# Making the projection's first chunk ready beside attention's last head

## The reference

```
ada = silu(c) @ W_ada + b_ada                     # six vectors of 576 for each of the 2 samples
h = modulate(layernorm(x), shift_msa, scale_msa)
q, k, v = split(h @ W_qkv + b_qkv)
o = softmax(q * 36**-0.5 @ k.T) @ v               # per head
x = x + gate_msa * (o @ W_proj + b_proj)
h = modulate(layernorm(x), shift_mlp, scale_mlp)
x = x + gate_mlp * (gelu(h @ W_fc1 + b_fc1) @ W_fc2 + b_fc2)
```

## Time and profile before

| what | value |
|---|---|
| median of 3 runs | 3662.12 us (3662.05 to 3669.55) |
| profiled execution, its own time | 3666.17 us |
| its span, first to last instruction | 3664.4 us |
| mean granted TensorE clock | 0.980 |
| TensorE busy | 3529.4 us (96%) |
| VectorE busy | 1886.7 us (51%) |
| ScalarE busy | 1560.5 us (43%) |
| GpSimd busy | 350.4 us (10%) |

### The profile page before, as it was taken

One profiled execution on the slowest core, in us unless ns is written; L12 is line 12 of the kernel. 1 busy time (PEld: TensorE's weight loads), 2 busy tenths in 40 slices (PEclk: granted clock), 3 DMA queues, 4 the chain that ended last, 5 costly groups with the idle time before them and its releaser, 6 DMA issues. The chain is left out here.

```text
span 3664.4 us, 46431 instructions
## 1 busy us (share of the span) xinstructions
PE 3529.4 (96%) x16996; PEld 2264.3 (62%) x16996; DVE 1886.7 (51%) x3413; ACT 1560.5 (43%) x2903; POOL 350.4 (10%) x277
## 2 busy tenths in 40 slices
PE   5999989999999999999999999997869999999999
PEld 4888844444444444444444444435759898988988
DVE  4445546666666666666666666624543323332232
ACT  2233246666665555665556555563551101111010
POOL 0000000111100000000000000005421010100000
PEclk8999989999999999999999999998989999999999
DMA  4455332121212111111112121105753222422221
GB/s 151 154 173 169 108 83 51 35 61 38 54 32 48 32 48 33 39 43 37 46 28 51 29 51 28 32 6 167 251 204 110 91 75 81 135 89 97 67 89 49
DMA packets 146160, 289.96 MB, mean 79 GB/s; under 512 B 18242, under 2 KB 44098, under 8 KB 139024
## 3 DMA queue, kind: packets, MB, share of 16 engines
q1 hardware_dynamic: 145940, 286.99, 25.5%
HBM read 181.52 MB, written 104.34 MB: 78 GB/s over the span
## 5 line engine op out<-in xcount | busy, mean ns | idle before, releaser
L965 DVE TENSOR_REDUCE q_mx<-b_sp 128x1 f32<-128x512 f32 x1984 | 1208.7, 681 | 627.9 <-PE b_sp L913 627.8
L1001 ACT ACTIVATE b_pt<-b_st 128x512 f32<-128x512 f32 x2048 | 1031.0, 624 | 805.7 <-PE b_st L931 805.7
L942 PE MATMUL b_op<-b_pt,b_vs 128*37 128x512 f32 x4096 | 929.4, 596 | 0.0
L913 PE MATMUL b_sp<-b_ks,b_qs 108*128 108x512 f32 x1344 | 572.5, 427 | 8.5 <-DMA b_ks<-qkl 7.6
L942 PEld LDWEIGHTS b_op<-b_pt,b_vs 128*37 128x37 f32 x4096 | 223.4, 113 | 537.9 <-issue 460.0
L931 PE MATMUL b_st<-b_qs,b_ks 110*128 110x512 f32 x1344 | 520.4, 409 | 1.8 <-ACT b_pt L1001 1.8
L1631 ACT ACTIVATE d_af<-d_pf,d_b 128x512 f32<-128x512 f32 x144 | 99.3, 690 | 749.2 <-PE d_pf L1553 749.1
L913 PEld LDWEIGHTS b_sp<-b_ks,b_qs 108*128 108x128 f32 x1344 | 254.3, 189 | 203.3 <-issue 168.4
L931 PEld LDWEIGHTS b_st<-b_qs,b_ks 110*128 110x128 f32 x1344 | 252.0, 188 | 151.7 <-ACT b_pt L1001 120.7
L1570 PE MATMUL d_pm<-d_vl,d_ah 128*128 128x288 f32 x1152 | 340.8, 296 | 0.0
L1571 PE MATMUL d_pm<-d_vh,d_al 128*128 128x288 f32 x1152 | 340.5, 296 | 0.0
(11 more groups left out here) (194 smaller groups left out, 4103.8 us busy)
## 6 DMA issues: line engine op xcount, KB each, us to landing
d_hh<-hth SPq DMA_DIRECT2D x16, 1280.0 KB, 6.5
qkh<-a_th SPq DMA_DIRECT2D x72, 256.0 KB, 2.0
qkl<-a_tl SPq DMA_DIRECT2D x72, 256.0 KB, 2.3
d_yi<-y SPq DMA_DIRECT2D x64, 288.0 KB, 3.0
d_hl<-htl SPq DMA_DIRECT2D x16, 1024.0 KB, 8.8
b_qs<-qkh SPq DMA_DIRECT2D x42, 288.0 KB
b_ks<-qkh SPq DMA_DIRECT2D x42, 288.0 KB
vd<-a_vx SPq DMA_DIRECT2D x8, 1184.0 KB, 6.3
```

Source lines behind the costliest of these rows:

```text
L913: e.matmul(sp[slot % 3][:, :], qs[i][0:108, qb * 128:qb * 128 + 128], ks[i][0:108, k4 * 512:k4 * 512 + 512], start=True, stop=True).then_i ...
L942: ins = e.matmul(op[blk % 2][64 * a:64 * a + VW, :], vs[h % 2][:, 2 * j + a, :], pt[g % NP][:, a * 512:a * 512 + 512], start=j == 0, stop= ...
L965: e.tensor_reduce(mx[:, k // 4, k % 4:k % 4 + 1], sp[slot % 3][:, :], AX.X, ALU.max).then_inc(s_mx, 1)
L1001: e.activation(pt[g % NP][:, a * 512:a * 512 + 512], st[x % 3][:, :], ACT.Exp, scale=SCALE).then_inc(s_p, 1)
```

## The change

Chunk 0's turns, its split and its bias additions move out of the projection and into attention's last head. `LAST` is step 248, the last head's first. In steps 249 to 253 TensorE makes one turn each, behind the 8 scores and ahead of the 16 products, in a bank of `sp`; VectorE multiplies, in place; ScalarE rounds behind the step's exponentials and evacuation. In steps 250 to 254 GpSimd adds a bias (the first four) and subtracts a low part, the first subtraction after a wait for the last reader of `qs0`. VectorE makes `sel` in step 248. GpSimd makes the pattern `who` (now in `x1`, which is still unused) and the gated bias at attention's start, from two bias loads there. SyncE loads chunk 0's tokens in step 246, and its x in step 249 once `sel` is complete. Attention no longer waits for its last stores; the projection does, in front of `load_sums(1)`. The tiles and semaphores that both phases use move into `Prefetch`. From the projection `turn(0) + bias(0)` are removed, and its first loads begin with chunk 1. What is computed is unchanged.

```diff
 class Prefetch:
+        self.sel = S.sb("sel", [48, KT, 128], R)
+        self.gb = S.sb("gb", [128, 2, C])
+        self.oi = S.sb("oi", [128, KT, CH])
+        self.x1 = S.sb("x1", [128, 4, C])
+        self.ah = S.sb("ah", [128, KT, CH], R)
+        self.al = qs0[:, :].rearrange("p (k t) -> p k t", k=4)
+    def load_tokens(self, e, c, oi, ot):
+        cols = slice(c * CH, (c + 1) * CH)
+        e.dma_start(oi[:, 0:4, :], ot[0:512, cols].rearrange("(k p) t -> p k t", p=128)).then_inc(self.s_a[c % 2], 16)
+        for r in (0, 64):
+            e.dma_start(oi[r:r + 64, 4, :], ot[512:C, cols]).then_inc(self.s_a[c % 2], 16)
+    def load_x(self, e, c, x1, xf):
+        rows = slice(c * CH, (c + 1) * CH)
+        e.dma_start(x1[:, :, :], xf[rows, :].rearrange("(t p) c -> p t c", p=128)).then_inc(self.s_x[c % 2], 16)
...
 def phase_attention
+    LAST = NBAT - 8
+        if LAST < b <= LAST + KT:
+            s.turn, s.turn_slot = b - LAST - 1, len(slots)
+            slots.append(("turn", s.turn))
+            elif kind == "turn":
+                e.wait_ge(W.s_u, n + 1)
...
     sync
             e.dma_start(W.gt[:, b, :], gd[0, b, :].partition_broadcast(128)).then_inc(W.s_gt, 16)
+            e.dma_start(W.gb[:, b, :], b_proj.partition_broadcast(128)).then_inc(W.s_bc, 16)
+            if s.b == LAST - 2:
+                W.load_tokens(e, 0, W.oi, ot)
+            elif s.b == LAST + 1:
+                e.wait_ge(W.s_sel, 5)
+                W.load_x(e, 0, W.x1, xf)
-            e.wait_ge(s_o[i], 32 * NBLK // 2)
+        e.wait_ge(W.s_a[0], 48)
+        e.wait_ge(W.s_x[0], 16)
+        e.wait_ge(W.s_bc, 32)
     tensor
+        def turn(kt, slot):
+            e.wait_ge(W.s_sel, 5)
+            e.wait_ge(W.s_rr, 32 * HCH)
+            slot_free(e, slot)
+            e.matmul(sp[slot % 3][:, :], W.sel[:, kt, :], W.rr[:, 0, :], start=True, stop=True).then_inc(W.s_ta, 1)
+            if s.turn is not None:
+                turn(s.turn, s.turn_slot)
     vector
+            if s.b == LAST:
+                select()
+            if s.turn is not None:
+                e.wait_ge(W.s_ta, s.turn + 1)
+                e.wait_ge(W.s_a[0], 48)
+                e.tensor_tensor(W.oi[:, s.turn, :], sp[s.turn_slot % 3][:, :], W.oi[:, s.turn, :], ALU.mult).then_inc(
+                    W.s_u, 1)
     scalar
+            if s.turn is not None:
+                e.wait_ge(W.s_u, s.turn + 1)
+                e.activation(W.ah[:, s.turn, :], W.oi[:, s.turn, :], ACT.Copy).then_inc(W.s_ah, 1)
     gpsimd
+        def low(kt):
+            e.wait_ge(W.s_ah, kt + 1)
+            if kt == 0:
+                e.wait_ge(s_st, 64 * (NH - 1))
...
+        def bias(t):
+            e.wait_ge(W.s_x[0], 16)
+            e.tensor_tensor(W.x1[:, t, :], W.x1[:, t, :], W.gb[:, 0, :], ALU.add).then_inc(W.s_xg, 1)
...
+        e.wait_ge(W.s_gt, 32)
+        e.wait_ge(W.s_bc, 32)
+        for b in range(2):
+            e.tensor_tensor(W.gb[:, b, :], W.gb[:, b, :], W.gt[:, b, :], ALU.mult).then_inc(W.s_gb, 1)
+            if LAST + 2 <= s.b < LAST + 2 + KT:
+                kt = s.b - LAST - 2
+                if kt < 4:
+                    bias(kt)
+                low(kt)
...
 def phase_proj
-        for p in turn(0) + bias(0):
-            yield p
     sync
-        load(0)
-        load_x(0)
-        e.dma_start(bb[:, :], b_proj.partition_broadcast(128)).then_inc(s_bc, 16)
         load(1)
+        for i in range(2):
+            e.wait_ge(W.s_o[i], 32 * 2 * NH)
         W.load_sums(e, 1, sm)
     vector, gpsimd: the making of sel, who and gb is removed here
```

More of the change, by code:

```diff
@@ L171, with __init__ @@
 class Prefetch:
[L175 removed]
+    def __init__(self, S, w0, qs0):
         self.stg = [S.sb(f"stg{i}", [128, C]) for i in range(2)]
@@ L182, in __init__ @@
         self.rr = S.sb("rr", [48, HCH, CH], R)
+        self.sel = S.sb("sel", [48, KT, 128], R)
[4 more added lines that the diff above has]
+        self.al = qs0[:, :].rearrange("p (k t) -> p k t", k=4)
+        self.oc = [S.sb(f"oc{i}", [VW, 512]) for i in range(2)]
+        self.s_o = S.sems("o", 2)
+        self.s_who, self.s_sel, self.s_bc, self.s_gb = S.sem("who"), S.sem("sel"), S.sem("bc"), S.sem("gb")
+        self.s_a, self.s_x, self.s_xg = S.sems("a", 2), S.sems("x", 2), S.sem("xg")
+        self.s_ta, self.s_u, self.s_ah, self.s_al = S.sem("ta"), S.sem("u"), S.sem("ah"), S.sem("al")
         self.s_gt, self.s_rz = S.sem("gt"), S.sem("rz")
@@ L296, in program @@
                 with ExitStack() as last:
-                    W = Prefetch(Scope(nc, last, "w", top), w0)
+                    W = Prefetch(Scope(nc, last, "w", top), w0, qs0)
                     with ExitStack() as ctx:
-                        phase_attention(nc, Scope(nc, ctx, "b", top), W, ident, qs0, ks0, mx, gd, W_proj, qkh, qkl, vd,
-                                        ot, sm)
+                        phase_attention(nc, Scope(nc, ctx, "b", top), W, ident, qs0, ks0, mx, gd, W_proj, b_proj, xf, qkh,
+                                        qkl, vd, ot, sm)
                     with ExitStack() as ctx:
                         phase_proj(nc, Scope(nc, ctx, "c", top), W, first, ident, qs0, ks0, adaT, eps, gd, xf, ot, sm,
-                                   W_proj, b_proj, W_fc1, hth, htl, y1)
+                                   W_fc1, hth, htl, y1)
             with ExitStack() as ctx:
@@ L778, in phase_attention @@
     ob = [A.sb(f"ob{i}", [VW, 512]) for i in range(2)]
-    oc = [A.sb(f"oc{i}", [VW, 512]) for i in range(2)]
+    oc = W.oc
     nm = A.sb("nm", [128, 16])
@@ L811, in phase_attention @@
                 s.last = todo // 64 - 1
+        s.turn = s.turn_slot = None
+        if LAST < b <= LAST + KT:
+            s.turn, s.turn_slot = b - LAST - 1, len(slots)
+            slots.append(("turn", s.turn))
         s.now = b - 1 if 0 < b <= NBAT else None
@@ L980, in max_rows, with select @@
             e.tensor_tensor(ml[:, :], src, mh[:, :].bitcast(F), ALU.subtract).then_inc(s_mh, 1)
+        def select():
+            e.memset(W.sel[:, :, :].bitcast(F), 0.0).then_inc(W.s_sel, 1)
+            e.wait_ge(W.s_sel, 1)
+            e.wait_ge(W.s_who, 3)
+            cols, who = W.sel[:, :, :].rearrange("h k c -> h (k c)"), W.x1[0:H, 0, :]
+            for r in (0, 32):
+                e.tensor_copy(cols[r:r + H, 0:C], who).then_inc(W.s_sel, 1)
+                e.tensor_copy(cols[r:r + H, C:640], who[:, 512:C]).then_inc(W.s_sel, 1)
         row_max(0)
@@ L1018, in scalar @@
                 W.w[i].high(e, kt, W.stg)
+            if s.turn is not None:
+                e.wait_ge(W.s_u, s.turn + 1)
+                e.activation(W.ah[:, s.turn, :], W.oi[:, s.turn, :], ACT.Copy).then_inc(W.s_ah, 1)
     def gpsimd(e):
+        def low(kt):
[3 more added lines that the diff above has]
+            if kt < 4:
+                e.tensor_tensor(W.al[:, kt, :], W.oi[:, kt, :], W.ah[:, kt, :].bitcast(F), ALU.subtract).then_inc(
+                    W.s_al, 1)
+            else:
+                e.wait_ge(W.s_al, kt)
+                e.wait_ge(W.s_xg, 4)
+                e.tensor_tensor(W.ah[64:128, kt, :], W.oi[64:128, kt, :], W.ah[64:128, kt, :].bitcast(F),
+                                ALU.subtract).then_inc(W.s_al, 1)
+                e.wait_ge(W.s_al, KT)
+        def bias(t):
+            e.wait_ge(W.s_x[0], 16)
+            e.tensor_tensor(W.x1[:, t, :], W.x1[:, t, :], W.gb[:, 0, :], ALU.add).then_inc(W.s_xg, 1)
         e.memset(W.rr[:, :, :].bitcast(F), 0.0).then_inc(W.s_rz, 1)
@@ L1023, in gpsimd @@
             w.zero(e)
+        who = W.x1[0:H, 0, :]
+        e.memset(who, 1.0).then_inc(W.s_who, 1)
+        e.wait_ge(W.s_who, 1)
+        e.affine_select(out=who, in_=who, compare_op=ALU.is_ge, fill=0.0, base=0, pattern=[[1, C]],
+                        channel_multiplier=-D).then_inc(W.s_who, 1)
+        e.wait_ge(W.s_who, 2)
+        e.affine_select(out=who, in_=who, compare_op=ALU.is_ge, fill=0.0, base=D - 1, pattern=[[-1, C]],
+                        channel_multiplier=D).then_inc(W.s_who, 1)
+        e.wait_ge(W.s_gt, 32)
+        e.wait_ge(W.s_bc, 32)
+        for b in range(2):
+            e.tensor_tensor(W.gb[:, b, :], W.gb[:, b, :], W.gt[:, b, :], ALU.mult).then_inc(W.s_gb, 1)
+        e.wait_ge(W.s_gb, 2)
         for s in plan:
@@ L1047, in phase_attention, with phase_proj @@
         block.gpsimd(gpsimd)
[L1050 to L1062, removed]
+def phase_proj(nc, A, W, first, ident, qs0, ks0, adaT, eps, gd, xf, ot, sm, W_fc1, hth, htl, y1):
+    gb, sel = W.gb, W.sel
+    oi = [W.oi, A.sb("oi1", [128, KT, CH])]
+    x1 = [W.x1, A.sb("x11", [128, 4, C])]
     xn = A.sb("xn", [128, 4, 640])
@@ L1069, in phase_proj @@
     rs = [A.sb(f"rs{i}", [128, 4]) for i in range(2)]
-    ah = [A.sb(f"ah{i}", [128, KT, CH], R) for i in range(2)]
-    al = [q[:, :].rearrange("p (k t) -> p k t", k=4) for q in (qs0, ks0)]
+    ah = [W.ah, A.sb("ah1", [128, KT, CH], R)]
+    al = [W.al, ks0[:, :].rearrange("p (k t) -> p k t", k=4)]
```

(2 more changed lines are left out.)

20 lines of the change are left out of this document (6 added, 14 removed).

## The result

The changed kernel takes 3649.4 us, the median of five runs (3643.3 to 3652.6). The kernel before, run beside it, had 3668.7 (3662.1 to 3671.8). The ratio is 0.9947, with a 95% interval of 0.9931 to 0.9963: 19 us less (14 to 25). The prediction said 21.1 us less, which lies within the interval, but it named 3641.0 with a range of 3635 to 3646, and 3649.4 lies outside it. Five more runs of the same kernel gave 3647.6 and a ratio of 0.9952.

A forecast was written before the change was run, and what follows sets the result against it. TensorE, busy in 96% of the span, was taken as the bound, its handover gap the opening: 21.2 removed less 1.75 for turns gives 19.5, plus 1.6 clock, 21.1 us; from 3662.12 that leaves 3641.0, range 3635 to 3646.

The forecast's parts named there:

- The base: Whole kernel before: median 3662.12 us, the profiled execution 4.05 above it; 21.1 less leaves 3641.0.
- The handover: Attention to projection: TensorE's gap falls from 25.0 to 3.8 us, 21.2 removed.
- 0.4 (... the crossing): Handover: from SyncE passing its wait for the last store to the next block, 0.4 us; could be dearer.
- the stores: Handover: not awaiting the landing of attention's last stores gives 1.7 us of the 21.2.
- The turns: Attention's last head: five turns lie on TensorE's path, 0.35 us each, 1.75 in all (bounds 1.15 and 2.45).
- The clock: Projection's chunk 0: clock probably falls again, low for 8.85 us; 3.9 us lost instead of 5.5, 1.6 gained.
- the rival of a clock that stays up: Handover: the clock does not fall, all 5.5 us come back, 25.0 saved, 3637.1 us; chance 0.19.
- The other rivals: Late chunk 1 tokens (3644.3 us); little of the gap goes away (3651.6, chance 0.05); slower (about 3676, chance 0.03).
- Chunk 1's tokens: Projection start: landing within 9.6 us is hidden, 12.9 costs 3.3; chance 0.13 shared with longest low clock and dear turns.
- never late: Last head: ScalarE rests 1.88 us before a batch's exponentials, covering its rounding; exponentials never wait for VectorE.
- The two broadcasts at attention's start: Attention's start: two bias broadcasts join SyncE's queue, GpSimd waits for them; cost nothing.
- The wait for the placed reciprocals: Projection's chunk 3: TensorE's 11.6 us wait for the second half moves along, neither mended nor worse.

The follow-up runs named there:

- before, unchanged again: The kernel before, unchanged, timed against itself and profiled a second time; 3668.9 us, ratio 1.0007.
- bias alone: The kernel before, with only the bias loaded and multiplied with the gates at attention's start; 3665.5 us, ratio 0.9994.
- changed again: The changed kernel, unchanged, run again with a second profile; 3647.6 us, ratio 0.9952.
- turns among the scores: The changed kernel, with each of the five turns behind the fifth of its batch's eight score matmuls, not the eighth; 3646.1 us, ratio 0.9947.
- closing waits ahead: The changed kernel, with SyncE's closing waits of attention in front of the wait for the last block, not behind its stores; 3645.8 us, ratio 0.9945.
- stores awaited: The changed kernel, with attention waiting for its last stores again; 3652.8 us, ratio 0.9965.
- turns back: The changed kernel, with the five turns and their split back at the start of the projection; 3653.3 us, ratio 0.9970.
- turns doubled behind: The changed kernel, with each of the five turn matmuls issued twice in a row, behind the scores; 3653.6 us, ratio 0.9965.
- turns doubled among: The changed kernel, with each turn matmul issued twice, among the scores; 3645.4 us, ratio 0.9945.
- kept busy: The changed kernel, with 18 idle matmuls of 512 columns behind attention's last product; 3644.4 us, ratio 0.9940.
- three together: The changed kernel with turns among the scores, 18 idle matmuls behind the last product and closing waits ahead of the last store; 3641.1 us, ratio 0.9937.
- three, 14 idle matmuls: The changed kernel with turns among the scores, closing waits ahead of the last store, and 14 idle matmuls instead of 18; 3640.4 us, ratio 0.9931.

## Why the prediction missed

**The base.** This is the step that failed: "It lies 4.05 above the median, 3662.12, from which 21.1 leaves 3641.0", with a range in which the scatter of the runs was only "rounded on". The kernel before takes between 3659 and 3672 us, its median over 11 or 17 runs is 3665 to 3669, and its profiled execution of 3666.17, read as 4 us too long, was an ordinary one. Of the 8.4 us between 3641.0 and 3649.4, 6.6 are the base (3668.7 less 3662.1) and 1.8 the saving (21.1 against 19.3), which its own interval of 14 to 25 does not tell from nothing. From 3667 the same 21.1 leave 3646, and a range with the scatter in it would have reached beyond 3650. The changed kernel itself scatters over 9 us.

Part of the scatter can be read off the traces. For each execution I summed the time in which TensorE worked at 0.50 in chunk 0 (the first 30 us of the projection) and from there to the first MLP matmul, and set it beside the projection's length (first projection matmul to first MLP matmul):

```
execution                   gap    low, chunk 0   low, later   projection
before                     25.02       12.7          16.8        221.3
before, unchanged again    25.13       12.9          16.4        221.8
bias alone                 20.40        3.2          11.4        214.9
changed                     4.48        4.6          12.0        216.3
changed again               4.48        8.1          17.3        220.3
turns among the scores      4.48        8.2          17.0        220.7
closing waits ahead         3.96        8.6          21.7        223.0
stores awaited              5.65        8.4          17.7        220.5
turns back                 13.05        4.1          11.8        216.3
turns doubled behind        4.47       12.6          11.9        219.5
turns doubled among         4.50        4.6          12.1        215.8
kept busy                   4.77        0.0          12.4        213.8
three together              4.76        0.0          17.1        215.4
three, 14 idle matmuls      3.98        0.0          10.2        213.2
```

A line through these points is 208.2 + 0.47 x (low in all), with a correlation of 0.99. Its slope is close to the 0.44 (1.91 / 4.38) that one unit with its turn loses for each microsecond at the low clock. So what the projection takes beyond the handover, 213 to 223 us, differs almost only by how long the clock stayed low. The rest of the kernel adds a few microseconds that I have not traced.

**The handover.** Right in place, a little off in size: 20.5 us out of the gap and not 21.2. The missing 0.65 is "0.4 (... the crossing)": SyncE's closing waits, all long met, had been hidden behind the stores' landing and came to light with the landing gone. Moving them ahead took 0.6 off the crossing and 0.5 off the gap. For the same reason the stores were worth 1.17 and not 1.7.

**The turns.** 2.2 us (5 x 0.43) where 1.75 was taken, within its bounds. But the sentence that TensorE passes through a batch "with no pause that an addition could use" was wrong: only at the place where the turn was put is there none. Eight scores of some 0.25 (3.47 / 14, the idle matmuls of the same shape) do not fill 3.57 us; they are spaced at 0.49 by ScalarE, and a turn among them is free. The earlier trace rows showed it, eight scores between 2434.21 and 2437.78 beside exponentials of 4.03 us.

**The clock.** Right in kind: low after the pause in all eight executions with a gap of 4 to 13 us and nothing to fill it, so the rival of a clock that stays up was never met unaided. The 8.85 us taken for its length stand beside 4.1 to 12.6 measured, 7.4 in the mean. At 0.44 lost for each low microsecond that is 3.2 us, 2.3 less than the 5.5 of before instead of 1.6 less. The Trainium skill, "TensorE: Matmul & The Clock Gate", section Loop structure matters more than you think, has matmuls kept back to back at the high clock; the trace agrees, since 14 idle matmuls, with 0.6 us of pause behind them, kept it there.

**The other rivals.** Chunk 1's tokens were waited for by VectorE (2.90 us) and not by TensorE, as the forecast had it. ScalarE rested 1.79 us ahead of the exponentials behind a turn with an evacuation, where it had rested 1.88, so it was never late. The two broadcasts at attention's start cost nothing that shows: GpSimd's products there ended at 499.2, its first sum came at 522.6. The wait for the placed reciprocals stayed.

The sum from measured terms: 20.5 - 2.2 + 2.3 = 20.6 us, against 19.3 by the first medians and 20.0 by the second. That it comes so near to the forecast 21.1 is partly luck: the gap and the turns were forecast 1.1 us too favourably, the clock 0.7 us too unfavourably.

## What to carry to other kernels

Before forecasting a time, look at how far runs of the same program lie apart; three runs and a profiled execution that disagree by 4 us say that the base is uncertain by as much, and the range has to hold it. Where an engine is paced by another, an added instruction can be free among the paced ones, as long as their pauses hold it, and is paid for behind them. When a wait is removed, ask what stood in its shadow, and where a handover leaves TensorE idle for some microseconds, a few matmuls that nobody reads can be worth more than the next microsecond cut from the gap.

## What the hardware showed unexpectedly

In chunk 0 the work done at the low clock until it came back fell into groups: 3.2 to 4.6 us, 8.1 to 8.6, and 12.6 to 12.9. The work of chunk 0 was the same in all. One and the same kernel, the changed one, had 4.6 in one execution and 8.1 in another, and gaps of 20.4 and 25.0 us had 3.2 and 12.7, so the length of the pause alone does not set it; what does is not shown. And the clock can fall while TensorE is at work: in the last head, three times in 14 executions, for about 3.4 us, each in the products behind a stretch of scores that ScalarE paces.
